# Turning the attention mask with DMAs instead of matmuls, and a rearranged start, in a one-core cross-attention kernel

## The reference

```python
Q = split_heads(x @ Wq.T + bq);  K = split_heads(ctx @ Wk.T + bk);  V = split_heads(ctx @ Wv.T + bv)
scores = einsum('bhqd,bhkd->bhqk', Q, K) / sqrt(32)
scores = where(mask[:, None] == 0, -1e9, scores)      # mask: (16, 512, 512), int32
attn = softmax(scores, axis=-1)
out = einsum('bhqk,bhkd->bhqd', attn, V) ... @ Wo.T + bo
y = out + x;  result = layernorm(y) * ln_g + ln_b
```

## Time and profile before

| | us |
|---|---|
| median of 3 runs | 1703.21 (1702.34 to 1704.61) |
| the profiled execution, its own time | 1699.52 |
| its span in the profile | 1697.7 |
| PE busy | 1645.0 (97%) |
| ACT busy | 1346.2 (79%) |
| POOL busy | 1294.2 (76%) |
| DVE busy | 1150.1 (68%) |
| DMA packets' time, as a share of 16 engines | 66.9% |

### The profile page before, as it was taken

How to read it: one execution, slowest core, us unless ns; L and a number is a source line. 1 busy time by engine, 2 the same in 40 slices (tenths; PEclk the granted TensorE clock), 3 DMA queues, 4 the chain that set the end, 5 groups by cost and what they waited for, 6 DMA issues and landing times.

```text
span 1697.7 us, 24843 instructions
## 1 busy us (share of the span) xinstructions
PE 1645.0 (97%) x7751; PEld 981.8 (58%) x7751; DVE 1150.1 (68%) x2835; ACT 1346.2 (79%) x1540; POOL 1294.2 (76%) x837
## 2 busy tenths in 40 slices
PE   6889999999999999999999999999999999999986
PEld 4546566565656656565665656556565665656532
DVE  6566766767666676766767676676776667676653
ACT  3388797888878888788888878787887878878773
POOL 5095787888778788778879778787877878877774
PEclk9999999999999999999999999999999999999997
DMA  8867685775777677586667668677676767756501
GB/s 302 268 190 199 174 228 181 215 201 187 206 207 207 185 202 221 163 234 187 204 192 209 201 172 238 181 205 200 190 205 204 207 182 203 221 160 192 166 9 69
DMA packets 180771, 329.62 MB, mean 194 GB/s; under 512 B 37408, under 2 KB 37408, under 8 KB 180640
## 3 DMA queue, kind: packets, MB, share of 16 engines
q1 hardware_dynamic: 180640, 328.03, 66.9%
HBM read 238.82 MB, written 89.13 MB: 193 GB/s over the span
## 4 chain that ended last, share of the span: by engine, by line
PE 90%; DMA 3%; DVE 2%; POOL 2%; issue 1%; ACT 1%; SPq 1%; POOLq 0%; DVEq 0%; ACTq 0%
PE proj_bank L968 43%; PE ctx_bank L892 14%; PE ring L861 13%; PE exp_banks L876 13%; PE ring L912 3%; DMA stack_scratch<-qk_lo 2%; POOL total L445 1%; PE ring L921 1%; PE ctx_bank L968 1%; DVE ring L686 1%; POOL total L453 1%; DVE qk_lo L714 1%; DMA bq_s<-bq_dram 0%; PE exp_banks L986 0%; DMA w_tile<-w_scratch 0%
## 5 line engine op out<-in xcount | busy, mean ns | idle before, releaser
L686 DVE CUSTOM_DVE_ANT_0 ring<-ring,bias 128x512 f32<-128x512 f32 x1024 | 691.1, 710 | 339.3 <-PE ring L861 339.2
L562 ACT ACTIVATE probs<-exp_banks 128x1024 f32<-128x1024 f32 x512 | 523.5, 1023 | 246.4 <-PE exp_banks L876 245.5
L536 ACT CAST exp_banks<-biasT 128x1024 f32<-128x1024 bf16 x512 | 520.7, 1017 | 24.1 <-ACT probs L562 0.8
L876 PE MATMUL exp_banks<-q_stack,k_stack 98*128 98x512 f32 x1024 | 374.4, 448 | 4.3 <-ACT exp_banks L536 4.3
L861 PE MATMUL ring<-k_stack,q_stack 96*128 96x512 f32 x1024 | 331.2, 401 | 13.8 <-DVE maxes L686 12.8
L453 POOL TENSOR_TENSOR total<-total,probs 128x1024 f32<-128x1024 f32 x126 | 297.4, 2381 | 9.4 <-POOL total L445 0.5
L445 POOL TENSOR_TENSOR total<-total,probs 128x2048 f32<-128x2048 f32 x63 | 289.8, 4600 | 7.5 <-ACT probs L562 0.7
L445 POOL TENSOR_TENSOR total<-probs 128x2048 f32<-128x2048 f32 x63 | 290.2, 4606 | 0.0
L892 PE MATMUL ctx_bank<-probs,v 128*32 128x512 f32 x2048 | 274.4, 608 | 0.7 <-DVE ctxT L747 0.7
L460 POOL CAST max_parts<-maxes 128x16 fp32r<-128x16 f32 x64 | 12.6, 198 | 322.9 <-DVE maxes L686 322.9
L876 PEld LDWEIGHTS exp_banks<-q_stack,k_stack 98*128 98x128 f32 x1024 | 194.1, 191 | 107.0 <-issue 69.6
(11 more groups left out here) (103 smaller groups left out, 1911.5 us busy)
## 6 DMA issues: line engine op xcount, KB each, us to landing
w_tile<-w_scratch SPq DMA_DIRECT2D x124, 512.0 KB, 4.4
k_stack<-stack_scratch SPq DMA_DIRECT2D x192, 256.0 KB, 5.3
q_stack<-stack_scratch SPq DMA_DIRECT2D x192, 256.0 KB, 7.2
stack_scratch<-qk_hi SPq DMA_DIRECT2D x128, 256.0 KB, 2.2
stack_scratch<-qk_lo SPq DMA_DIRECT2D x128, 256.0 KB, 2.5
raw<-cT_dram SPq DMA_DIRECT2D x64, 256.0 KB, 4.8
raw<-xT_dram SPq DMA_DIRECT2D x64, 256.0 KB, 5.0
raw<-mask_dram SPq DMA_DIRECT2D x64, 256.0 KB, 4.3
```

The source lines that it names most:

```text
L536: nc.scalar.copy(exp_banks[:, 2 - 2 * wave:4 - 2 * wave, :], biasT[:, kc:kc + 1, :].to_broadcast([P, 2, L])).then_inc(seeded, 1)
L562: nc.scalar.activation(probs[:, u % PS, 2 - 2 * wave:4 - 2 * wave, :], exp_banks[:, 2 - 2 * wave:4 - 2 * wave, :], ACT.Exp).then_inc(exps, 1)
L686: nc.vector.tensor_tensor_reduce(out=ring[:, n % 2], in0=ring[:, n % 2], in1=bias[:, c], scale=1.0, scalar=LOWEST, op0=ALU.subtract, op1=A ...
L876: mm = nc.tensor.matmul(exp_banks[:, h], k_stack[0:3 * D + 2, at, kc * P:(kc + 1) * P], q_stack[0:3 * D + 2, at, :], start=False, stop=Tru ...
```

## The change

Four things are edited together.

1. `turn_mask` moves from PE to SP: four DMAs with transposition, 128x128 bf16 each, from `bias` straight to `biasT`, at units 12, 13, 14 and 15 of the sequence before, on new semaphores `mask_turned`. DVE's copy, the ring's mask items and the identity on POOL go. The sign that the identity gave is now given by ACT's seed (a copy with scale -1).
2. `MADE` becomes 8: the weight tiles K2, Q2, K3 and Q3 of the first sequence are split by POOL at units -6, -5, -3 and -2, not loaded from `w_scratch`.
3. In the start SP issues Wo, the constants and the K part of `w_scratch` at unit -5 in place of -8, the Q part at -1 in place of -7, the raw inputs of the second sequence at -1 and 0 in place of -4.
4. Fewer filler matmuls keep the PE awake in the start (`AWAKE`), and they stand behind the second half of a projection; DVE makes the first Q tile's weights before it scales the bias; the product of bv and Wo moves from unit -5 to -2.

```diff
-MADE = 4
+MADE = 2 * NG
+AWAKE = {-12: 9, -10: 4, -9: 4, -8: 4, -7: 3, -6: 6}
-    MASKS = {13: 0, 14: 1, 15: 2, 1: 3}
+    MASKS = {12: 0, 13: 1, 14: 2, 15: 3}
+    MAKE = {-6: ("K", 0, 2), -5: ("Q", 0, 2), -3: ("K", 0, 3), -2: ("Q", 0, 3)}
...
-        s, kc = (y + 3) // UPS, self.MASKS.get(y % UPS)
+        s, kc = (y + 4) // UPS, self.MASKS.get(y % UPS)
...
+            def turn_mask(s, kc):
+                sp.wait_ge(bias_ready, (s + 1) * NC)
+                if s >= 1:
+                    sp.wait_ge(seeded, 2 * (s * UPS - NC + kc) + 2)
+                for c in range(NC):
+                    sp.dma_start_transpose(biasT[:, kc, c * P:(c + 1) * P],
+                                           bias[:, c, kc * P:(kc + 1) * P]).then_inc(
+                                               mask_turned[kc], FULL)
...
-                if y == -8:
+                if y == -5:
                     load_weight(WoT, wo[:, :, :], wo_loaded)
...
                     stack("Q", PLAN.stack_group(y))
+                if PLAN.mask(y):
+                    turn_mask(*PLAN.mask(y)[1:])
                 if PLAN.max_group(y) is not None:
                     move_maxes(PLAN.max_group(y))
...
-                if y == -7:
+                if y == -1:
                     scratch(1, (total[:, :, :], rows[:, :, :]), wq_split, wq_scratch)
...
-                if y == -4:
+                if y == -1:
                     for t in range(NK):
                         load_raw(1, 0, t)
+                if y == 0:
                     for t in range(3):
                         load_raw(1, 1, t)
...
+                if y in PLAN.MAKE:
+                    make_weights(pool, nc.gpsimd, PLAN.MAKE[y])
...
-                    act.wait_ge(ring_free, PLAN.ring["M", s, kc] + 1)
+                    act.wait_ge(mask_turned[kc], FULL * NC * (s + 1))
...
-                nc.scalar.copy(exp_banks[:, 2 - 2 * wave:4 - 2 * wave, :],
-                               biasT[:, kc:kc + 1, :].to_broadcast([P, 2, L])).then_inc(seeded, 1)
+                nc.scalar.activation(exp_banks[:, 2 - 2 * wave:4 - 2 * wave, :],
+                                     biasT[:, kc:kc + 1, :].to_broadcast([P, 2, L]),
+                                     ACT.Copy, scale=-1.0).then_inc(seeded, 1)
...
-                ring_wanted = PLAN.sums(y) or PLAN.mask(y)
+                ring_wanted = PLAN.sums(y)
...
-                if PLAN.mask(y):
-                    copy_mask(*PLAN.mask(y)[1:])
...
-                if PLAN.mask(y):
-                    turn_mask(*PLAN.mask(y)[1:])
```

More of the change, by code:

```diff
@@ L82, in __init__ @@
             for item in (self.score(y, 0), self.score(y, 1), self.score(y, 2), self.score(y, 3),
-                         self.mask(y), self.sums(y)):
+                         self.sums(y)):
                 if item:
@@ L214, in xattn_program @@
         tail_done, tail_biased = sem("tail_done"), sem("tail_biased")
+        mask_turned = [sem(f"mask_turned{n}") for n in range(NC)]
         mask_scaled, o_biased = sem("mask_scaled"), sem("o_biased")
@@ L237, in by_tile, with make_weights @@
             return t.rearrange("p n (t c) -> p t n c", t=NK).bitcast(FP32R)
+        def make_weights(eng, ops, tile):
+            i = PLAN.qk[tile]
+            src = (wq_raw if tile[0] == "Q" else wk_raw)[:, :, tile[2]]
+            if i >= WS:
+                eng.wait_ge(proj_done, PLAN.no[PLAN.qk_list[i - WS]] + 1)
+            if i:
+                eng.wait_ge(first_lo, i)
+            ops.tensor_copy(w_tile[:, i % WS, 0], src).then_inc(first_hi, 1)
+            eng.wait_ge(first_hi, i + 1)
+            ops.tensor_tensor(w_tile[:, i % WS, 1], src, w_tile[:, i % WS, 0].bitcast(FP32),
+                              ALU.subtract).then_inc(first_lo, 1)
         def last_bank(n):
@@ L367, in _ @@
                         stack(tile[0], 0)
-                if y == -7:
+                if y == -1:
                     scratch(1, (total[:, :, :], rows[:, :, :]), wq_split, wq_scratch)
-                tile = PLAN.tile(y + (1 if y < -4 else 2))
+                tile = PLAN.tile(y + 2)
                 if tile and tile[0] in "QK":
@@ L417, in _ @@
             nc.gpsimd.memset(masked_t[:, :], MASKED).then_inc(consts_made, 1)
[L418 to L424, removed]
             def split_lo(seq, use, t):
@@ L496, in _ @@
             for y in range(START, END):
-                if y == -10:
+                if y == -9:
                     low_weights(wk_raw, by_tile(ctxT[:, 0:NG]), by_tile(q_stack[:, 2 * HG:3 * HG]),
@@ L628, in _ @@
         def _(dve):
[L630 to L637, removed]
-                                        w_tile[:, i % WS, 0].bitcast(FP32),
-                                        ALU.subtract).then_inc(first_lo, 1)
             def split(src, hi, lo, done):
@@ L656, in _ @@
             dve.wait_ge(wq_scaled, 1)
-            make_weights(("Q", 0, 0))
+            make_weights(dve, nc.vector, ("Q", 0, 0))
+            dve.wait_ge(qk_bias_loaded, 2 * FULL)
+            nc.vector.tensor_scalar(bq_s[:, :], bq_s[:, :], SCALE, None,
+                                    ALU.mult).then_inc(bq_scaled, 1)
             def prologue(y):
                 if y == -9:
-                    make_weights(("K", 0, 1))
+                    make_weights(dve, nc.vector, ("K", 0, 1))
                 if y == -8:
-                    make_weights(("Q", 0, 1))
+                    make_weights(dve, nc.vector, ("Q", 0, 1))
                     dve.wait_ge(wv_loaded, FULL)
                     split(probs[:, 2], wv_hi[:, :, :], wv_lo[:, :, :], wv_split)
-                if y == -6:
+                if y == -3:
                     dve.wait_ge(consts_loaded, 4 * FULL)
@@ L669, in prologue @@
                         [P, NG, P])).then_inc(bv_wide, 1)
-                if y == -3:
+                if y == -1:
                     dve.wait_ge(bv_wo, 1)
@@ L826, in _ @@
         def _(pe):
-            pe.wait_ge(consts_made, 7)
+            pe.wait_ge(consts_made, 4)
             def keep_awake(count):
@@ L912, in sum_probs @@
                     mm = nc.tensor.matmul(ring[h * D:(h + 1) * D, n % 2], ones[:, :], total[:, h],
-                                          start=True, stop=True)
-                mm.then_inc(ring_filled, 1)
-            def turn_mask(s, kc):
-                n = PLAN.ring["M", s, kc]
-                pe.wait_ge(bias_ready, (s + 1) * NC)
-                pe.wait_ge(ring_free, n - 1)
-                for c in range(NC):
-                    mm = nc.tensor.matmul(ring[:, n % 2, c * P:(c + 1) * P],
-                                          bias[:, c, kc * P:(kc + 1) * P], ident_bf[:, :],
                                           start=True, stop=True)
@@ L995, in _ @@
                     projection(PLAN.tile(y - 1), 1)
+                if y in AWAKE:
+                    mm = keep_awake(AWAKE[y])
+                    if y == max(AWAKE):
+                        mm.then_inc(banks_written, 1)
                 shifted_scores(y, 0)
```

28 lines of the change are left out of this document (5 added, 23 removed).

## The result

1783.41 us median (1778.17 to 1790.72) against 1703.21 (1701.13 to 1704.61), five runs each: ratio 1.0471, 95% interval 1.0448 to 1.0493. The prediction, 1686.5 in 1677 to 1725, missed: 80 us slower, not 17 faster. The profiled execution is the slowest of the five (1790.72, span 1788.9); the traces of the experiments too are of one execution each, and those lie up to 6.4 us from their medians, so sums made from a trace can differ from the medians by that much.

What follows compares the result with a forecast made beforehand. PE was taken to bound the steady part, transfers the start. Steady saving 15.0 - 1.1 - 3.2 = 10.7 us plus 6.0 in the start made 16.7; 1703.2 - 16.7 = 1686.5 us, range 1677 to 1725.

Steps and rivals of the forecast that it cites:

- What bounds the kernel: PE bounds some 15 sequences, a microsecond of PE worth a microsecond; the start hangs on transfers.
- Turns taken off PE: Units 13, 14, 15 and 1: PE saves 1.0 us a sequence, 15.0 us over 15 sequences.
- Issue: SP in units 12 to 15: each transpose takes 0.45 us to issue, four 1.8, hidden in 3.4 us free at unit 12.
- rival 3: Unit 12: issues above 0.85 us each on SP delay K's halves directly; at 1.4 each 1722 us; chance 0.10.
- Queue: Unit 12: four transposes between stacks and K's halves delay the halves by t, costing 1.1 + 3.2 us in all.
- t: Queue time of four transposes ahead of K's halves: taken as 0.5 us, bounds 0.42 and 5.6; total gain 24.7 - 16 t.
- Rival 2: Unit 12 of every sequence: the queue holds transposes one by one ahead of K's halves; 1768 us; chance 0.19.
- The Trainium skill: Two pages on transposing DMAs: 1309 ns a block, 5.2 us for four; or 350 to 400 GB/s, t 0.3 to 0.4.
- The start: K(0,1)'s and K(0,2)'s halves land sooner, unit 0 starts at about 71.5 for 77.70: 6 us gained, bounds 0 and 20.
- rival 1: The start gives nothing: deferred 2 MiB and raw inputs collide with group 2's stacks; 1692.5 us; chance 0.08.

Runs made afterwards that it cites:

- pairs kernel: Also called 11: the changed kernel whole, but one transpose turns 128 x 256 into two blocks, 8 a sequence in place of 16: 1692.18 us, ratio 0.9938.
- Experiment 4: The changed kernel with the four transposes of a unit issued behind the halves of its tile instead of ahead of them: 1860.45 us, ratio 1.0919.
- 6: The kernel before, PE's and DVE's turn kept, plus 11 stores of 4 KB on SP in each of units 12 to 15 of 15 sequences: 1768.79 us, ratio 1.0389.
- plain copies: The changed kernel with each transposing DMA replaced by an ordinary one of the same block, mask untransposed: 1704.90 us, ratio 0.9996.
- 7: The changed kernel whole, the same 16 transposes a sequence spread over SP's idle times, two ahead of K's halves of unit 12: 1744.56 us, ratio 1.0239.
- 9: The kernel before with its start as it was, the mask turned by the spread transposes of 7 alone: 1743.43 us, ratio 1.0239.
- 8: As 7, but no transposes ahead of K's halves of unit 12; 4 at the end of unit 12, 2 at the end of unit 13: 1783.18 us, ratio 1.0477.
- Experiment 2: The changed kernel with the mask turned by PE and copied by DVE as before, so only the start's changes are left: 1698.69 us, ratio 0.9975.
- experiment 1: The kernel before with only the mask's turn moved to SP's transposing DMAs, start as before: 1782.93 us, ratio 1.0468.
- 12: The kernel before with its start, the mask turned by pair transposes alone, 8 a sequence: 1692.70 us, ratio 0.9938.

## Why the prediction was wrong

**What bounds the kernel**: right. PE bounds the steady part, and every microsecond that it waited was paid.

**Turns taken off PE**, 15.0 us: right in size where nothing is late. The best third group went from 24.8 to 24.2 and the fourth from 25.8 to 25.5, 0.9 a sequence against 1.0. In the mean of the pairs kernel 0.3 a sequence are left of it.

**Issue**: the step that failed. I took 0.45 us each, the pace of ordinary issues, and let 3.4 us of free time hide four. They take 1.23 each. This alone would not have given the result: in rival 3's formula it makes (4.92 - 3.4 + 0.5) x 16 - 24.7 = +7.6 us, 1711. The second half of the step was wrong by more: I priced the issue at K's halves of unit 12, and let those of units 13 to 15 go because maxima and mask are wanted late. Behind these, on the same queue, stand the stacks of unit 0. Four groups are 20 us of SP in the 24.6 between two stack issues; these stacks went out 33 us after those of unit 12, and PE waited 40 us for them (of 62). Experiment 4 shows it with K's halves out of it (third group 25.0, fourth 35.5), and 6 without any transpose.

**Queue**, t = 0.5: the mechanism was right, the size too small. In unit 12 of the changed kernel the last of the four transposes lands 1.2 us behind the last stack read in nine of 13 sequences (the first and the last left out), 2.2 to 2.6 in the other four. K's low half lands 13.9 us behind SP's first stack issue (means of 13; before 12.5). Of these 1.5 us 1.2 are SP's: the low half is issued 8.4 to 9.4 us behind the stacks, for 7.1 to 7.5; its own landing took 4.5 to 6.7, for 4.4 to 6.0. Where SP was not late, in the plain copies, the landing was 1.1 longer (6.1 for 5.1). With t = 1.1 the sum would give 1696: the term alone leaves a small gain and does not explain the loss. That the queue's order is the landing order holds at this place; in the whole trace of before 43 of 1290 neighbours on SP's queue land the other way round. Rival 2, the transposes one by one in the queue, which I held likeliest of the slow ones, didn't occur: four issued 1.3 us apart in the pairs kernel (956.8 to 960.7) landed at 962.1, 962.5, 962.7 and 963.1, though each carries two blocks. Near K's halves the queue is tight as argued: two blocks ahead of them go with a third group of 26.1 and 25.3 (7, 9), none with 24.8 (8).

**Rival 3** had the mechanism, at 0.10, and the wrong place and price: 1722 for 1783. Its sign, transposes issued over more than 0.85 us each, is what was seen.

**The Trainium skill**: "VectorE: DVE Perf Modes", The three transpose paths, gives 1309 ns for a block by DMA; the row shows 1232 ns, but as the time that the issuing engine is held, which I had read as time in the queue. "Advanced Engine Details and Errata", X-Bar Transpose (TRN2), agrees with the trace in that the transfer is about as fast as a regular one: landing 3.5 us, as the plain copies' 3.5. Its 350 to 400 GB/s, which made t 0.3 to 0.4, are not what these small blocks reached: 0.13 MB in 1.2 us are some 110 GB/s (an estimate). That section says nothing of the issue.

**The start**: 6 us expected, unit 0 at 71.5. Measured in the changed kernel 77.72, and then the stacks of group 2 were late and PE stood until 98.41 in this chain:

```profile
74.27 1.24 SPq L354
75.55 1.23 SPq L354
76.82 1.24 SPq L354
78.11 1.24 SPq L354
...
88.00 10.32 DMA q_stack<-stack_scratch
98.41 1.19 PE ring L854 x2
```

This looks like rival 1, but the deferred writes and raw inputs are not what makes it late. Experiment 2 has them too, and SP issues the stacks of group 2 at 73.03 (before 73.09, here 85.20); experiment 1 has them not, and there the stacks go out at 89.04 and the first inversion is as late. It is again SP's time, four groups of transposes ahead of these stacks. Rival 1's collision is in the landing: from the first of these issues to the last landing it is 12.8 us in experiment 2 and 11.2 before, 13.1 here and 10.1 in experiment 1.

Without transposes the start gives 4.3 us (experiment 2, interval 2.0 to 6.5); with any of them nothing (9 against 7, 12 against 11). The step that failed there is the drain of the queue ahead of K(0,2)'s halves: I had them land at 57.9, and without transposes they landed at 61.44. Wo was issued at 38.76, so 6.0 MB took 22.7 us, some 266 GB/s (an estimate) and not 311. In the pairs kernels the chain of waits lies in SP's queue from about 66 (new start) and 60 (old) to the stacks of group 2, and these go out at 79.97 with the new start and 79.30 with the old; the first inversion is at 105.66 and 105.47. The new start also has the lower granted clock from 60 to 117, 0.88 in experiments 2 and 11 for 0.97 before and in 12, with fewer filler matmuls; what this costs was not tried. Where the 4.3 us of experiment 2 lie is only in part known: its first inversion is 2.5 sooner, and its profiled execution is no shorter than that of before (spans 1700.3 and 1697.7).

## What to carry to other kernels

Price a DMA on two accounts: the transfer, and the time in which it holds the engine that issues it. Sum the second over everything that the queue must issue between two deadlines, not only up to the first; the instruction that goes late may be some units on and of another kind. Where an issue takes no longer for a larger transfer, as here for twice the bytes, widen the transfer before spreading it. And a needed transfer must not stand behind large ones that nobody waits for yet.

## What was not expected of the hardware

- A transposing DMA held SP 1.20 to 1.23 us whether it moved 32 or 64 KB; an ordinary copy of the same 32 KB block 0.60, other ordinary issues 0.43 (medians). Single ordinary ones took much longer: four reads of raw inputs behind two writes of 1 MiB held SP 4.5 us in the start, 1.9 before.
- A block of 32 KB issued behind six reads of 256 KB landed 6.2 us later; four transposes of 64 KB issued behind K's halves landed in 2.4 to 5.3 and 0.2 to 0.4 us from each other.
- After 3.6 us without work PE ran at a granted clock of 0.59 for 4.2 us: this wait costs about half as much again. In the changed kernel PE waited over 3 us seven times between 200 and 1600, and the granted clock of the 4 us behind was 0.50 to 0.68 each time; in experiment 1 it was so seven times of eight, and 1.00 once, after 3.35 us.
